# Moving the stores of a streaming pass from the sync engine's queue to ScalarE's

## The reference

```python
# layer 0: a strided grouped convolution x -> d (8, 256, 64, 64); channel groups by k-means on d[0];
# a gate per image and group from a small mixture fit; then
pre_up = gate * d + d
x = _bilinear_up_x2(repeat(pre_up, 2, axis=1) * w_up) + sx
# layer 1: attention in a basis of 64 products of cosines; everything up to `out` is small
out = einsum('bvk,bkn->bvn', WvxP, out / lamdv) + out_bias
return gamma * out.reshape(x.shape) + x
```

## Time and profile before

| | |
|---|---|
| three runs | 2755.03, 2759.83 and 2767.95 us; median 2759.83 us |
| profiled execution | 2754.47 us, span 2752.7 us |
| busy in the span | PE 85%, DVE 78%, PE weight loads 58%, ACT 43%, POOL 27% |
| DMA, whole span | 923.89 MB, mean 336 GB/s |
| queue q1 (issued by SP) | 887.16 MB |
| queue q10 (issued by ACT) | 33.59 MB, all in `first_pass` |

### The profile page before, as it was taken

One profiled execution on the slowest core, in us unless ns is written; L12 is line 12 of the kernel. 1 busy time (PEld: TensorE's weight loads), 2 busy tenths in 40 slices (PEclk: granted clock), 3 DMA queues, 4 the chain that ended last, 5 costly groups with the idle time before them and its releaser, 6 DMA issues.

```text
span 2752.7 us, 52146 instructions
## 1 busy us (share of the span) xinstructions
PE 2336.0 (85%) x20710; PEld 1585.5 (58%) x20710; DVE 2140.2 (78%) x2317; ACT 1185.1 (43%) x3193; POOL 754.3 (27%) x388
## 2 busy tenths in 40 slices
PE   7999999999994654866999888898888988888776
PEld 2222222222224422435988888888787887877776
DVE  3899898898995314553999989898887887888776
ACT  0000001000012001324777777776766766766764
POOL 2111111111100000001444444444433343344343
PEclk9999999999997676987999999999999999999998
DMA  9999999999975255006999999999999999999998
GB/s 363 388 388 389 389 388 344 388 389 389 389 239 208 122 199 61 0 18 241 396 417 417 415 408 403 410 405 395 382 375 374 377 379 378 374 386 371 369 373 330
DMA packets 495971, 923.89 MB, mean 336 GB/s; under 512 B 212737, under 2 KB 213121, under 8 KB 493314
## 3 DMA queue, kind: packets, MB, share of 16 engines
q1 hardware_dynamic: 356482, 887.16, 84.9%
q10 hardware_dynamic: 139264, 33.59, 5.6%
HBM read 615.00 MB, written 303.56 MB: 334 GB/s over the span
## 4 chain that ended last, share of the span: by engine, by line
DMA 36%; PE 10%; DVE 3%; ACT 3%; issue 2%; SPq 1%; POOL 1%; DVEq 0%; ACTq 0%
DMA out<-second_x 29%; PE second_o L1253 6%; DMA second_dd<-downsampled 5%; DMA second_x<-in_x 2%; DVE second_x L1477 1%; DVE second_left L1026 1%; ACT second_mid L1342 1%; PE second_mid_t L1223 1%; PE second_st L1113 1%; SPq L1059 1%; ACT second_left L1354 1%; POOL second_left L1026 1%; DVE second_mid L1458 1%; ACT second_part L1342 0%; PE second_zt_t L1236 0%
## 5 line engine op out<-in xcount | busy, mean ns | idle before, releaser
L1253 PE MATMUL second_o<-second_right,second_left 128*128 128x128 f32 x8192 | 1074.2, 280 | 114.9 <-issue 44.1
L1253 PEld LDWEIGHTS second_o<-second_right,second_left 128*128 128x128 f32 x8192 | 991.7, 195 | 149.3 <-issue 140.7
L1026 POOL TENSOR_TENSOR second_left<-second_mid_copy,second_coef_rep 64x1024 f32<-64x1024 f32 x256 | 608.6, 2377 | 1333.5 <-ACT second_mid_copy L1363 1317.8
L1477 DVE SCALAR_TENSOR_TENSOR second_x<-second_o,second_shift,second_x 128x512 f32<-128x512 f32 x1024 | 734.5, 738 | 213.0 <-PE second_o L1253 111.1
L278 PE MATMUL first_conv<-first_x,first_band 64*64 64x512 f32 (+2 forms) x6144 | 548.9, 616 | 19.7 <-DMA first_x<-in_x 19.7
L252 ACT ACTIVATE first_staged<-first_conv 128x512 f32<-128x512 f32 x128 | 76.5, 597 | 740.7 <-issue 462.8
L278 PEld LDWEIGHTS first_conv<-first_x,first_band 64*64 64x64 f32 (+1 forms) x6144 | 166.6, 118 | 393.4 <-issue 385.8
L217 DVE TENSOR_TENSOR first_product<-first_freq,first_cols 128x4096 f32<-128x4096 f32 x64 | 283.2, 4424 | 125.0 <-PE first_freq L302 122.8
L1342 ACT ACTIVATE second_mid<-second_dd,all_inter 128x128 f32<-128x128 f32 x1024 | 313.3, 388 | 89.6 <-DMA second_dd<-downsampled 87.5
L202 POOL TENSOR_TENSOR first_band<-first_shift,first_w_all 128x576 f32<-128x576 f32 x128 | 145.5, 1158 | 648.3 <-PE first_conv L278 641.1
L1342 ACT ACTIVATE second_part<-second_dd,all_inter 128x128 f32<-128x128 f32 x1024 | 313.2, 388 | 3.2
(11 more groups left out here) (218 smaller groups left out, 1316.5 us busy)
## 6 DMA issues: line engine op xcount, KB each, us to landing
first_x<-in_x SPq DMA_DIRECT2D x128, 2048.0 KB, 21.5
second_x<-in_x SPq DMA_DIRECT2D x256, 1024.0 KB, 14.2
out<-second_x SPq DMA_DIRECT2D x256, 1024.0 KB, 16.2
downsampled<-first_staged ACTq DMA_DIRECT2D x512, 64.0 KB, 10.6
gather_d<-downsampled SPq DMA_DIRECT2D x16, 2048.0 KB, 15.9
second_dd<-downsampled SPq DMA_DIRECT2D x64, 512.0 KB, 14.8
second_p<-in_p_cols SPq DMA_DIRECT2D x1, 4096.0 KB
gates_ft<-all_wv SPq DMA_DIRECT2D x64, 32.0 KB, 5.7
```

What stands on the lines that cost most here:

```text
L1026: return eng.tensor_tensor(left[a][rows, odd:HALF:2, :, :].rearrange("p n (t s) g -> p n t s g", t=T), turned[rows, :, :, :].unsqueeze(3). ...
L1253: last = nc.tensor.matmul(ob[n][:, r, :], left[a][:, r, n, :], right[a][:, r, :], start=True, stop=True)
L1477: nc.vector.scalar_tensor_tensor(out=xt[i][:, n // S, n % S, rows, :], in0=ob[n][:, :, :], scalar=shift[:, n:n + 1], in1=xt[i][:, n // S, ...
```

## The change

The store goes from SP's instruction list to ACT's, onto ACT's own queue. ACT issues both halves of a chunk in the even unit that follows the chunk, after that unit's `copy` and `weight`. SP keeps the loads, which wait for the same semaphore as before (the landing of the store of chunk `m - 1`), with no store between them. The wait of a store, for the last addition to its half, is the same. The store of the last chunk follows after ACT's last step.

```diff
 @block.sync
-                def store(b, m, t):
-                    i = m % XBUF
-                    sp.wait_ge(added[t * S + S - 1], b * UNITS + 2 * m + 2 + FREE)
-                    sp.dma_start(ov[b, t, :, :, m * ROWS2 * W:(m + 1) * ROWS2 * W],
-                                 xt[i][:, t, :, :, :].rearrange("g s h w -> g s (h w)")).then_inc(y_out[i][t], 16)
...
                     for t in range(T):
-                        if u % 2 == 1:
-                            store(b, m, t)
                         if u % 2 == 1 and (more or m + AHEAD < CH2):
                             load_image(b, m + AHEAD, t)
 @block.scalar
+                def store(b, m):
+                    i = m % XBUF
+                    for t in range(T):
+                        act.wait_ge(added[t * S + S - 1], b * UNITS + 2 * m + 2 + FREE)
+                        act.dma_start(ov[b, t, :, :, m * ROWS2 * W:(m + 1) * ROWS2 * W],
+                                      xt[i][:, t, :, :, :].rearrange("g s h w -> g s (h w)")).then_inc(y_out[i][t], 16)
...
                     if more or m + 2 < CH2:
                         weight(b, m + 2, u % 2)
+                    if u % 2 == 0 and b + u > 0:
+                        store(b if u else b - 1, (m - 1) % CH2)
                 batches(act, step, prologue)
+                store(B - 1, CH2 - 1)
```

## The result

The changed kernel takes 2680.31 us (median of 4 runs, 2676.33 to 2683.35) against 2762.98 us for the kernel before on the same occasions: 0.9703 of it, 95% interval 0.9674 to 0.9731.

The account below looks back on a forecast made before the run. DMA bandwidth was taken to bound the second pass. DMA 1372 us, nearly tied with computing 1365, plus 46 us of waits gave 1418 against 1448.5, so 2729 us for the kernel; range 2684 to 2830 us.

Parts of the forecast that it names:

- The forecast for the pass: Second pass: DMA rate of 410 GB/s with stores and loads in two queues, against 388 GB/s on average before.
- engines that store together: Second pass: slow stretches read as DMA engines all storing at once, 225 and 238 GB/s in the nearest rows.
- the signs that the prediction named: Second pass: q10 carries 268 MB more, GB/s near 410 without a fall, data waits well under 184 us, landings under 16.2 us.
- ACT's issues cost 0.79 us a chunk, 101 us: ACT between weights and next copy: two store issues take 1.32 us, partly in 0.53 us idle; range 69 to 298 us.
- 1365 us for the computing: Second pass: computing without data waits, 1264.3 us, plus 101 us for ACT's store issues.
- the DMA's 1372 us: Second pass: 562.6 MB at 410 GB/s; bounds 1349 us at 417 GB/s and 1537 us at 366.
- the 46 us: Second pass: a quarter of the 184.2 us of data waits, kept because the two nearly equal limits don't hide wholly.
- The 1264.3 us: Second pass: 1448.5 us less 184.2 us of ACT's waits for dd and DVE's for x; 9.88 us a chunk.
- Stores later, at no cost: Second pass: first halves go out 4.7 us later, second 0.3 us earlier; possible 42 us in all, taken as nothing.
- The first, the same rate: Second pass: queues don't matter, 562.6 MB stay at 388 GB/s, kernel 2760 us; chance 0.22.
- The second rival: ACT between weights and next copy: issues at 2.86 us a pair make the pass 1562 us, kernel 2874 us; chance 0.19.
- The third, a poor rate for mixed packets: Second pass: loads and stores mixed packet by packet go slowly throughout, 1537 us, kernel 2849 us; chance 0.14.

Follow-up runs that it names:

- stores alone: No computing: loads four chunks once, then stores from them 128 times, 268 MB of stores; 686.05 us, 405 to 408 GB/s after the first slices.
- The streams with the extra load: Three kernels without computing (single stores and loads alternating, pairs, two queues), each with one 4 KB load a chunk added from ACT: 1470.65, 1307.49 and 1320.57 us.
- the stream beside the matmuls: Stores and loads alternating in one queue without the kernel's computing, with 8192 independent f32 matmuls added: PE runs to 1836.04 us, transfers done after some 1340 us.
- the streams: Kernels without computing that move x through four buffers to the output: one queue alternating 1284.79 us, one queue in pairs 1287.14, two queues 1283.02.
- the alternating stream: No computing: x through four buffers to the output, one queue, order store, load, store, load; 1284.79 us, with one 4 KB load a chunk added 1470.65 us.
- the stream in pairs: No computing: x through four buffers, one queue, both stores of a chunk ahead of both loads; 1287.14 us, with one 4 KB load a chunk added 1307.49 us.

## Why the prediction was right in direction and wrong in size

**DMA is the limit, and the change lifts its rate to about 410 GB/s: the right number by luck, for a wrong reason.** The forecast for the pass was 410, the mean of the windows is 411. But it was put down to a second queue and to engines that store together. One queue with both stores ahead of both loads does the same (0.9712 beside 0.9703), and stores alone go at 406. Most of the signs that the prediction named came true, but they do not tell the reasons apart: with one queue reordered q10 carries no store, a store lands after 17.5 us, ACT and DVE still wait 170.9 us for data, and the gain is there. What the full kernels show in its place is the order: where single stores and loads alternate in one queue, the rate falls or stays low at a full DMA share (366 GB/s late in the kernel before); in pairs, or with the change, it does not (405 to 418 in the windows from 1400 to 2600 us). The change ends the alternation, and that is its gain. The streams with the extra load, one run each, show one condition under which the order matters: an uneven load on the engines. That the kernel's own instruction fetches are this load is made likely by the stream beside the matmuls, but it was not shown in the full kernel.

**ACT's issues cost 0.79 us a chunk, 101 us: wrong, and this is the step that failed.** They cost nothing that shows in the time: ACT issues them beside its own scalings, the idle time of the copy stays 0.53 us in the unit shown, and 256 more issues change nothing. From that price came 1365 us for the computing, from that the tie with the DMA's 1372 us, and from the tie the 46 us that were put on top. Without it the sum is the DMA's 1372 us alone, and the pass took 9 us more than that.

The other term of the computing was too small. The 1264.3 us were the pass less the waits for data of two engines, but such waits can't simply be subtracted: for the change that gives 1380.6 - 81.2 = 1299 us, for one queue reordered (1294.82 to 2676.44 us) 1381.6 - 170.9 = 1211 us. The kernel without dd's loads, where 1.2 us of such waits are left, shows what the computing takes, from the same scaling to the last addition:

```profile
1294.17 2.38 POOL L1026 TENSOR_TENSOR second_left<-second_mid_copy,second_coef_rep 64x1024 f32<-64x1024 f32 x1 [5.12 <-ACT second_mid_copy L1368]
...
2603.96 4.89 DVE L1482 SCALAR_TENSOR_TENSOR second_x<-second_o,second_shift,second_x 128x512 f32<-128x512 f32 x6 [0.68 <-DMA second_x<-in_x]
```

That is 1314.7 us, 50 more than 1264.3 and still 57 below the DMA's 1372. With the predicted price on top it would be 1416 us, above the DMA; so it is the price that failed.

**The sum, measured.** The prediction's start of the pass, the scaling at 1292.53 us, was in truth the pass's third; the first was at 1278.34 us, so that the stretch has 127 chunks and not 128. From third scaling to last addition both kernels can still be compared:

```profile
1293.62 2.38 POOL L1026 TENSOR_TENSOR second_left<-second_mid_copy,second_coef_rep 64x1024 f32<-64x1024 f32 x1 [5.12 <-ACT second_mid_copy L1362]
...
2670.75 3.43 DVE L1479 SCALAR_TENSOR_TENSOR second_x<-second_o,second_shift,second_x 128x512 f32<-128x512 f32 x4 [0.66 <-PE second_o L1244]
```

2674.18 - 1293.62 = 1380.6 us, against 1448.5 before and 1418 forecast: 37 of the 49 us that are missing. Another 4 us are the tail behind the last addition (11.7 us before, 7.4 after), which was taken as unchanged, and the pass came 1 us later. The rest is that the prediction put the median 5.4 us above the profiled execution, as before, and it lies 3.0 us below.

**Stores later, at no cost: right.** In the unit shown the first went out at 2008.36 us, 2.4 us after the chunk's last addition and not 4.9, since ACT issues ahead of its scalings:

```profile
2003.86 2.05 DVE L1479 SCALAR_TENSOR_TENSOR second_x<-second_o,second_shift,second_x 128x512 f32<-128x512 f32 x3
```

A store lands 10.7 us after its issue and not 16.2, which more than pays for it, and issuing it in the chunk's own unit changes nothing (2676 us).

**The rivals.** The first, the same rate, is what the kernel with dd alone on ACT's queue shows (0.9976); it fell for the change. The rule of the Trainium skill (DMA: Bandwidth & Descriptors, section Issuing engines are not separate DMA queues), that issuing from several engines saves only issuing time, agrees with the streams, 1283 us on two queues and 1285 on one, and with the 0.9712 that one queue reordered gives. Nearly all of this change's 3% came from the order, then, and not from the second queue. The second rival, ACT's issues as the bound, fell with their price. The third, a poor rate for mixed packets, fell with 421 GB/s on two queues.

**Left open.** Why alternating single transfers suffer from an uneven load, and pairs and two queues hardly, is not seen in these views: the share stays near 1 and only the GB/s fall. What loads the engines unevenly in the full kernel, and whether dd's loads have a part in it, was not shown either: the one full kernel without them has no slide, but there the computing is the limit.

## What to carry to other kernels

Read DMA share and GB/s side by side: a full share with a falling rate can mean, as here, that the transfers can still go faster, and the order in which one queue gets them is a cheap thing to try, ahead of a second queue. A stream that keeps its rate alone may lose it beside a small uneven load, so try an order with such a load added. Before a price is put on a DMA issue on a computing engine, look whether that engine has work queued that runs beside it. And what the computing takes without its waits is better read from a kernel that has no such waits than found by subtracting them.

## What was not expected of the hardware

A DMA issue of 0.54 to 0.63 us on ACT took no time from the activations around it, and appeared in the trace ahead of activations that stand before it in the code. An extra load of 4 KB for each 4 MB of traffic took the alternating stream from 421 to about 345 GB/s; the same bytes made the stream in pairs 1.6% longer and the one on two queues 2.9%. Stores alone ran at 406 GB/s, a little below the 421 of stores and loads together.
